# Products on zeros in front of TensorE's waits, in the first tile's first steps and the last tile's closing ones

## What is computed

```python
x = x + cross_attention_0(layernorm(x), ctx)       # one head of 256, 257 context rows per batch
x = x + causal_attention(layernorm(x))             # one head of 128
x = x + feed_forward(layernorm(x))                 # quantised weights and activations, 1024 wide, gelu
x = x + cross_attention_1(layernorm(x), ctx)       # 16 heads of 16
x = x + local_attention(layernorm(x))              # 5 neighbours, one head of 256
x = x + experts(layernorm(x))                      # router over 8 experts, top 2, each 256 -> 1024 -> 256
```

## Time and profile before

| | us |
|---|---|
| three runs | 1514.6, 1517.16, 1522.25 (median 1517.16) |
| the profiled execution | 1516.38, of which its span is 1514.6 |
| first phase, until the routing's first step on VectorE | 932.8 |
| routing, until the first expert block's transposes | 932.8 to 985 |
| experts | 985 to 1514 |
| TensorE busy | 1386.4 (92% of the span) |
| TensorE's mean granted clock | 0.959 |

### The profile page before, as it was taken

How to read it: one execution, slowest core, us unless ns; L and a number is a source line. 1 busy time by engine, 2 the same in 40 slices (tenths; PEclk the granted TensorE clock), 3 DMA queues, 4 the chain that set the end, 5 groups by cost and what they waited for, 6 DMA issues and landing times. The chain is left out here.

```text
span 1514.6 us, 51179 instructions
## 1 busy us (share of the span) xinstructions
PE 1386.4 (92%) x19679; PEld 1179.2 (78%) x19680; DVE 852.4 (56%) x2933; ACT 829.0 (55%) x2393; POOL 626.2 (41%) x1265
## 2 busy tenths in 40 slices
PE   4879999999999999999999985299999999999997
PEld 3557777777777777777777763199999999999996
DVE  3578888888888888888888864811111111111110
ACT  0378898988888898988888871111111111111110
POOL 0132434343343424343343320046555555555554
PEclk6799999999999999999999996589999999999999
DMA  9423343434343433434342003446655665566653
GB/s 300 139 68 93 106 118 92 117 96 127 93 131 93 115 110 100 116 94 122 93 118 72 13 13 133 168 149 189 183 173 176 187 186 178 173 182 192 181 174 80
DMA packets 94784, 198.57 MB, mean 131 GB/s; under 512 B 14561, under 2 KB 49058, under 8 KB 84482
## 3 DMA queue, kind: packets, MB, share of 16 engines
q1 hardware_dynamic: 75698, 173.97, 37.1%
q0 software_dynamic: 15904, 18.66, 5.8%
q10 hardware_dynamic: 2992, 3.28, 0.6%
HBM read 177.88 MB, written 17.99 MB: 129 GB/s over the span
## 5 line engine op out<-in xcount | busy, mean ns | idle before, releaser
L1678 ACT ACTIVATE heT<-ps 128x512 f32<-128x512 f32 x142 | 84.8, 597 | 434.9 <-PE ps L1644 434.9
L1644 PEld LDWEIGHTS ps<-xeT,w_block 128*128 128x128 f32 x2272 | 267.5, 194 | 5.2 <-DVE xeT L1575 0.9
L1644 PE MATMUL ps<-xeT,w_block 128*128 128x128 f32 x2272 | 268.2, 277 | 1.0 <-DVE xeT L1555 0.5
L833 ACT ACTIVATE x_prob<-ps,x_nmax 128x257 f32<-128x257 f32 x512 | 237.4, 476 | 47.6 <-DVE x_rinv L1210 38.4
L1630 PE MATMUL ps<-w,heT 128*128 x1136 | 256.8, 379 | 0.0
L1630 PEld LDWEIGHTS ps<-w,heT 128*128 128x128 f32 x1136 | 210.5, 190 | 25.6
L1206 DVE TENSOR_REDUCE x_nmax<-ps 128x2 f32<-128x514 f32 x256 | 167.0, 684 | 19.9 <-PE ps L595 13.2
L1692 POOL TENSOR_TENSOR rt_hold<-constants 128x1 f32<-128x1 f32 x213 | 82.5, 387 | 219.3 <-DMA out<-ye,to_ix 134.0
L603 PE MATMUL ps<-constants,x_prob 128*128 128x128 f32 x1024 | 148.7, 277 | 20.4 <-ACT x_prob L833 19.8
L921 POOL TENSOR_TENSOR query_var_eps<-query_moments,epsilon 128x1 f32<-128x1 f32 x32 | 6.1, 190 | 370.3 <-DVE query_moments L1075 370.3
L837 ACT ACTIVATE x_probT<-ps 128x512 f32<-128x512 f32 x256 | 140.4, 600 | 25.3 <-PE ps L603 24.8
(11 more groups left out here) (283 smaller groups left out, 2841.0 us busy)
## 6 DMA issues: line engine op xcount, KB each, us to landing
w_block<-in_m_w SPq DMA_DIRECT2D x71, 1024.0 KB, 5.1
context<-in_cT SPq DMA_DIRECT2D x128, 257.0 KB, 3.1
context<-in_cn SPq DMA_DIRECT2D x128, 256.0 KB, 4.2
w<-in_m_w SPq DMA_DIRECT2D x8, 1024.0 KB, 12.0
xin<-in_x SPq DMA_DIRECT2D x32, 128.0 KB, 3.0
lastq<-in_lastq SPq DMA_DIRECT2D x32, 128.0 KB, 3.0
context<-in_lastk SPq DMA_DIRECT2D x32, 128.0 KB, 3.8
out<-x SPq DMA_DIRECT2D x32, 128.0 KB, 1.7
```

What stands on the lines that cost most here:

```text
L833: A(p1[u % 2][:, r, :], ps[:, r, 0:KEYS], ACT.Exp, bias=nmax1[u % 2][:, r:r + 1], accum_out=rsum1[u % 2][:, r:r + 1]).then_inc(e1_ok.handl ...
L1644: t = mm(ps[:, 2 * b + n, f * P:(f + 1) * P], w1[b][:, k, lo:lo + P], xeT[b][:, k, :], start=k == 0, stop=k == H - 1)
L1678: A(heT[b][:, n * FK // 2:(n + 1) * FK // 2, :].rearrange("p k t -> p (k t)"), ps[:, 2 * b + n, :], ACT.Gelu).then_inc(heT_ok.handle, 1)
```

## The change

A helper `keep_busy(n, b)` issues n products of `zero`: 128x128 weights, 64 moving columns, into the first 64 columns of bank b. Nobody reads them, and nobody waits for them. 24 of them take the place of the 17 products with 128 moving columns at the start. For tile 0 they stand ahead of the waits of the seven first steps: 14, 8, 4, 24, 3, 3 and 3, into bank 3. For tile 31 they stand ahead of the waits of `s1_norm_T` (16), `s1_q` (4), `s1_v_scores` (4), `s1_probs_T` (9), `s1_values` (4), `ro_norm_T` (16) and `ro_logits` (4), into bank 0. These are 59 products in the first tile and 57 in the last. Nothing else is changed.

```diff
--- before.py
+++ after.py
@@ -392,8 +392,13 @@
             mm = nc.tensor.matmul
             tr = nc.tensor.transpose
             pe.wait_ge(zero_ok, 1)
-            for n in range(17):
-                mm(ps[:, 6, 0:P], zero[:, 0:P], zero[:, 0:P], start=True, stop=True)
+
+            def keep_busy(n, b):
+
+                for _ in range(n):
+                    mm(ps[:, b, 0:P // 2], zero[:, 0:P], zero[:, 0:P // 2], start=True, stop=True)
+
+            keep_busy(24, 3)
             pe.wait_ge(fold_in, 48)
             for h in range(H):
                 for k in range(H):
@@ -442,6 +447,8 @@
                 return t
 
             def c0_norm_T(t):
+                if t == 0:
+                    keep_busy(14, 3)
                 W(pe, norm_s["cross0"], t, "norm")
                 W_bank(pe, (t - 5, (dve_s["self1"], "q")), (t - 1, (dve_s["cross0"], "att")))
                 for h in range(H):
@@ -449,6 +456,8 @@
                 i.then_inc(pe_s["cross0"].handle, 1)
 
             def c0_q(t):
+                if t == 0:
+                    keep_busy(8, 3)
                 W(pe, act_s["cross0"], t, "normT")
                 for h in range(H):
                     i = product(bank(B["c0_q"])[:, h * P:(h + 1) * P], [(x0_A[:, k, h * P:(h + 1) * P], xnT["cross0"][:, k, :]) for k in range(H)])
@@ -456,6 +465,8 @@
 
             def c0_scores(t):
 
+                if t == 0:
+                    keep_busy(4, 3)
                 m = t % RING
                 W(pe, act_s["cross0"], t, "q")
                 W_bank(pe, (t - 1, (dve_s["self0"], "masked")))
@@ -476,6 +489,8 @@
 
             def c0_values(t):
 
+                if t == 0:
+                    keep_busy(3, 3)
                 W(pe, act_s["cross0"], t, "probsT")
                 W_bank(pe, (t - 1, (dve_s["self0"], "x")))
                 for k in range(KT):
@@ -643,6 +662,8 @@
                 product_in_halves(bank(B["s1_out"])[:, 0:D], [(outT[t % 2][:, k, :], x1_W[:, k, :]) for k in range(H)]).then_inc(pe_s["self1"].handle, 1)
 
             def s1_norm_T(t):
+                if t == tiles - 1:
+                    keep_busy(16, 0)
                 W(pe, norm_s["self1"], t, "norm")
                 W_bank(pe, (t + 4, (dve_s["cross0"], "att")), (t + 3, (dve_s["self0"], "x")), (t - 2, (dve_s["router"], "logits")))
                 for h in range(H):
@@ -650,28 +671,38 @@
                 i.then_inc(pe_s["self1"].handle, 1)
 
             def s1_q(t):
+                if t == tiles - 1:
+                    keep_busy(4, 0)
                 W(pe, act_s["self1"], t, "normT")
                 for h in range(H):
                     i = product(bank(B["s1_q"])[:, h * P:(h + 1) * P], [(a1_A[:, k, h * P:(h + 1) * P], xnT["self1"][:, k, :]) for k in range(H)])
                 i.then_inc(pe_s["self1"].handle, 1)
 
             def s1_v_scores(t):
+                if t == tiles - 1:
+                    keep_busy(4, 0)
                 W(pe, dve_s["self1"], t, "q")
                 W_bank(pe, (t + 3, (act_s["ffn_in"], "inT")), (t + 1, (f1_ok, 2)), (t - 1, (dve_s["self1"], "masked")))
                 product(bank(B["s1_v_scores"])[:, 0:D], [(xnT["self1"][:, k, :], full["a1_Wv"][:, k, :]) for k in range(H)])
                 product(bank(B["s1_v_scores"])[:, D:D + P], [(q1T[:, k, :], xnT["self1"][:, k, :]) for k in range(H)]).then_inc(pe_s["self1"].handle, 1)
 
             def s1_probs_T(t):
+                if t == tiles - 1:
+                    keep_busy(9, 0)
                 W(pe, act_s["self1"], t, "probs")
                 W_bank(pe, (t + 1, (f1_ok, 4)), (t - 1, (dve_s["self1"], "x5")))
                 tr(bank(B["s1_probs_T"])[:, 0:P], prob["self1"][:], ident[:]).then_inc(pe_s["self1"].handle, 1)
 
             def s1_values(t):
+                if t == tiles - 1:
+                    keep_busy(4, 0)
                 W(pe, act_s["self1"], t, "probsT")
                 mm(bank(B["s1_values"])[:, 0:D], probT["self1"][:, 0, :], val["self1"][:], start=True, stop=True).then_inc(pe_s["self1"].handle, 1)
 
 
             def ro_norm_T(t):
+                if t == tiles - 1:
+                    keep_busy(16, 0)
                 W(pe, norm_s["router"], t, "norm")
                 W_bank(pe, (t + 4, (dve_s["ffn"], "x")), (t + 1, (dve_s["self1"], "q")), (t - 1, (dve_s["router"], "logits")))
                 for h in range(H):
```

## The result

| | before | after |
|---|---|---|
| median of 20 runs each, us | 1520.64 | 1524.42 |
| lowest and highest, us | 1514.6 to 1523.4 | 1516.6 to 1535.3 |
| standard deviation, us | 2.3 | 5.0 |
| the profiled execution, us | 1516.38 | 1531.14 |

One run of before took 3027 us; it is left out of the range and the deviation (without it the median is 1520.20). The ratio is 1.0039, with a 95% interval of 1.0023 to 1.0054, so the change costs 5.9 us (3.5 to 8.2). It was forecast as 1519.4, +3.0 us, and "within 0.5%".

The account below looks back on a forecast made before the run. The prediction saw pipeline fill, steady part, last tile's close, routing and experts in series, with only fill and close touched. From the profiled 1516.38 us, fill 0 and close +3.0 gave 1519.4 us, range 1512 to 1532.

Parts of the forecast that it names:

- The price of a filler: Every filler: the weight load sets its time, 0.22 us a product at full clock and 0.44 at half, 64 columns or 128.
- The cover up to `c0_max(0)`: Fill: a delay of up to 7.2 us before the first scores' maximum costs nothing, as it starts only at 32.00.
- (a) to (d): Fill, burst and groups of 14, 8 and 4 up to the scores: together +1 to +12, taken as +5 to +8.
- (a): Burst at the start, 48 records for 34: +0.5 if the clock rises; otherwise ends at 11.6, folds some 2.5 us longer.
- The 24: Fillers before tile 0's probabilities' transposes: clock rises within the first third, 7.1 us from about 28, +2.
- Threes and the gain behind them: Fill, before values, attention transposes and out product: +0.4, or +2.4 at half clock; out product and first folds then return -2.7.
- The close: Last tile's steps up to the routing, at full clock throughout: +3.0 us; +11 or +18 with the clock low.
- first 16: Close, before the transposes of `s1_norm_T(31)`: overruns its wait by +2.4 us at full clock, +5.9 at half.
- second 16: Close, before the transposes of `ro_norm_T(31)`: +1.9 us.
- Slow fillers: Rival: fillers don't raise a low clock and cost 0.44 each; 1527 in the close alone, 1538 in both; chance 0.27.
- Full hold: Rival: fillers raise the clock in the burst and it never falls in fill or close; 1512; chance 0.15.
- No effect: Rival: clock state as before and the 16s hide in longer waits; 1516 to 1517; chance 0.06.

Follow-up runs that it names:

- e1_head: The change with fillers only at the start and in tile 0, none in the last tile; ratio 1.0023 against before, +3.5 us.
- e4_no16: The whole change with the last tile's two groups of 16 cut to 4 each; ratio 1.0009 against before, +1.4 us.
- e2_tail: The change with the last tile's fillers only, the start as before; ratio 1.0038 against before, +5.8 us.
- e5_narrow: The whole change with the same counts, but 32 columns of weights per filler instead of 128; ratio 0.9978 against before, -3.3 us.
- e3_wide: The whole change with the same counts, but 128 moving columns per filler instead of 64; ratio 1.0005 against before, +0.8 us.
- e10_fithead: Before plus tile 0 groups of 8, 8, 4, 24, 2, 2, 2 with 128 moving columns, burst still 17; ratio 0.9992 against before, -1.2 us.
- e8_no24: The first tile's part of the change alone, without the group of 24 ahead of the probabilities' transposes; ratio 1.0124 against before, +18.8 us.
- e12_shift: Before plus 42 products of one column (168 instructions) in the wait of `c0_probs_T(0)`; ratio 1.0141 against before, +21.4 us.

## Why the prediction was right, and where it was off

*The price of a filler* was right, and it decided the sign: 0.22 us a record at half clock (10.51 us for 48) and 0.11 at full (3.76 us for 32), 64 columns or 128. By the Trainium skill's formula for a load, 107 ns for 128 columns with no term for the clock (TensorE: Matmul & The Clock Gate, LDWEIGHTS), the 24 products would have taken 5.1 us, an estimate; they took 10.48.

*The cover up to `c0_max(0)`* was right, and the maximum stayed where it was. The +5 to +8 for (a) to (d), measured as +6.8 on the scores, was luck in part. It was taken for a cold burst and the rest mixed; in after nearly all was at half clock, for which the sum gave +12. Two errors cancelled: the burst did end at 11.58, the cold bound's 11.6, and the folds 4.0 us late, but only 1.8 us of that reached the group of 14 (16.66 for 14.90), as VectorE had waited 2.33 us there for a DMA anyway. The sum had added all of (a)'s 5.8.

*The 24* is the term that was mis-sized. I took a rise of the clock within the first third of the group, 7.1 us and +2; in after and e1_head it didn't come at all, and the group ended at 42.26, near the forecast's own bound of 41.9. In e4_no16 the clock was at full when the group began: 5.55 us, +4.4, as it started at 32.02 behind cold groups. So the +2 lies under both outcomes. The start was wrong in both: 31.98 is 4 us later than the "about 28" that I put down, and the +5 to +8 of the same paragraph already gave 30 to 33. *Threes and the gain behind them*: in after the out product starts 1.2 us later relative to the transposes (between the +0.4 and the +2.4 of the two clocks), and the product and the folds return 0.9 and 1.7, as expected. By tile 2's probabilities the fill is 7.7 us late in after and 8.1 in e1_head, but only 0.7 (79.47 for 78.75) in e4_no16, where the clock rose. So the forecast's 0 is near one of two outcomes, and e1_head's ratio, +3.5 us (0.9 to 5.9), is what executions cost on average.

*The close* step by step, on after's trace (expected at full clock, then measured): first 16 +2.4, +3.4; 4 before the queries +0.2, +1.1; 4 before values +0.1, +1.6; values, scores and the 9 together -1.4, -1.3; 4 before the values product +0.3, +0.3; second 16 +1.9, +2.0; last logits -0.5, -0.6. Sum +3.0, +6.5. All that is off lies between 928.3 and 935.1, where the clock was at half; "full clock from there to 930" was wrong, as the clock fell inside the fillers that were to hold it. (The prediction also reads the rise in before's close as 917.5; a grant of 0.92 over 917.0 to 917.5 puts it at 917.1. Nothing in the sum hangs on it.) The second 16, at full throughout, came out within 0.1 us.

*The rivals.* "Slow fillers" (1524 to 1530 in the close alone, 1538 in both) is what the traced execution comes nearest to, at 1531.1, with +7.7 in the fill and +6.5 in the close for its +11 and +11; of 20 runs of after ten lie at 1525 or above, two of them at 1535. I gave it 0.27 as though it were one state of the program. By the traces with the same stream it is something that an execution falls into or not, and the median lies between the cases. That fits the spread of the runs, 5.0 us where before's is 2.3, but no more than one execution of after was traced. "Full hold" fell: fillers with 128 columns of weights and 64 moving ones raised the clock neither in the burst (all five traces with such a burst: 10.5 us for 48 records) nor in e2_tail's first 16. "No effect" fell with the ratio.

*The level.* The median is 5.0 us above the 1519.4. Before's own median, over 20 runs, came out 4.3 above the traced execution on which the sum was made, and the medians are 3.8 apart where I had 3.0; that accounts for the 5.0. The ratio, which compares runs on the same chips, puts the difference at 5.9 and so above the forecast's 3.0, which its interval (from 3.5) leaves out: the direction and the order of the loss were right, and its size is about twice the forecast.

*Open:* what sets the moments at which the clock rises and falls, in the fill and in the close, in one execution and not in another. This reaches into the part between fill and close too, which takes 838.5 to 839.1 us in before, after and e4_no16 and 840.8 to 842.7 in the others of normal length, a 3 us difference as large as the effects told apart here. Most of it lies behind tile 31's first probabilities' transposes: from there to tile 29's logits it takes 84.0 to 84.6 us in the first three and 86.6 to 87.7 in seven of the others, which all have one or two stretches at half clock between 862 and 888 us, where the first three are at full up to 880 at least. In e2_tail and e5_narrow it is 85.0 and 85.5, and about 2.5 us more are lost between tiles 2 and 5. So the 3.0 us that e3_wide and e10_fithead gained in the fill were spent again there, in these traces.

## What to carry to other kernels

Cost a filler by what it really occupies, at the slow clock, since that is the clock at which it is meant to be used: if its load takes longer than its moving columns, moving fewer of them saves no time (64 for 128 here). Make a group no longer than the wait that it stands in (4 for 16 here: 0.9 us at full clock for the 0.92 of the first wait, though still 1.8 at half), and read afterwards that the real step has idle time in front of it again. And when a kernel changes by 1% in a place that the edit didn't touch, test the length of the instruction stream first: an equal number of nearly free instructions reproduces it or doesn't, and the records between two stalls and the packets ahead of them say the rest.

## What the runs showed of the hardware

- 168 more instructions ahead of an unchanged steady part cost 19 to 21 us (e8_no24, e12_shift), in stalls that are multiples of 256 records apart in e8_no24 (within one) and end 1.2 to 1.6 us after a 16,384-byte packet on the instruction queue; 200 or 264 more have no such stall before 850 us.
- In after the clock fell at 928.3 with TensorE busy without a gap since 925.2, from 925.6 on with products that move 64 columns per load of 128. Products of zeros with 128 columns did raise it, in the burst (48 records in 7.86 us in e3_wide) and in the close.
- A product with 32 columns of weights and 64 moving ones costs 0.11 us a record at half clock and 0.06 at full (e5_narrow: 48 records in 5.27 and in 2.87 us).
- The granted clock of the first slice can't be trusted: the profile counts the stretch up to the first change that it has (13.5 us in after, 30.1 in e4_no16) as full, while the burst's records there are 0.22 us apart.
